# Cross-attention and ternary FFN on one core: the last slot's quantising order, and tile 31 transposed by TensorE

## The reference

```python
# x (8,512,512) f32, ctx (8,64,512), mask (8,64); layernorm without gain, eps 1e-5
x = x + xattn(layernorm(x), ctx, mask)      # softmax over 64 context rows, scale 1/sqrt(512)
x = x + ffn(layernorm(x), w1, g1, w2, g2, w3, g3)
# linear_bit(x, w, g) = act_quant(rmsnorm(x, g)) @ ternary(w).T
#   act_quant: scale = 127 / max|x| of a row; y = round(x * scale) / scale
#   ternary:   s = mean|w|;  wq = round(tanh(w / s)) * arctanh(s)
def ffn(x, ...):
    h = silu(linear_bit(x, w1, g1)) * linear_bit(x, w2, g2)    # 512 -> 2048
    return linear_bit(h, w3, g3)                               # 2048 -> 512
```

## Time and profile before

| | |
|---|---|
| median of 3 runs | 484.7 us (482.98 to 485.55) |
| the profiled execution, its own time | 481.35 us |
| its span in the profile | 479.6 us |
| mean granted TensorE clock | 0.982 |
| busy: PE, DVE, ACT, POOL | 86%, 85%, 73%, 70% |
| DMA transposes into `q3T` | 64, median 3.2 us from issue to landing |

### The profile page before, as it was taken

The page is one execution under the profiler, slowest core; times in us unless marked ns, Lnnn a source line. Parts: engine busy times, 40 slices in busy tenths (PEclk is TensorE's granted clock), DMA queues, the critical chain, the costliest instruction groups (busy, mean ns, idle before and its releaser), DMA issues. The chain is left out here.

```text
span 479.6 us, 8317 instructions
## 1 busy us (share of the span) xinstructions
PE 412.8 (86%) x1910; PEld 195.2 (41%) x1910; DVE 406.7 (85%) x913; ACT 351.0 (73%) x608; POOL 337.5 (70%) x535
## 2 busy tenths in 40 slices
PE   0634777799999999999999999999999999799964
PEld 0511532234634463446344644464345534344421
DVE  3496796989999999999999999999999999987650
ACT  1678669986898769876988698868887876565560
POOL 0146837897877787788778878778777878877540
PEclk9999996999999999999999999999999999999988
DMA  7997661444566455745584557456744334535324
GB/s 265 392 392 249 200 250 22 131 90 110 133 155 165 96 109 153 186 87 124 139 179 87 118 156 175 87 116 179 175 88 111 77 79 92 107 72 99 73 68 87
DMA packets 112616, 67.98 MB, mean 142 GB/s; under 512 B 102864, under 2 KB 102992, under 8 KB 108880
## 3 DMA queue, kind: packets, MB, share of 16 engines
q1 hardware_dynamic: 112592, 67.72, 54.0%
HBM read 34.14 MB, written 8.39 MB: 89 GB/s over the span
## 5 line engine op out<-in xcount | busy, mean ns | idle before, releaser
L488 POOL TENSOR_TENSOR stageB<-stageB,g3b 128x512 f32<-128x512 f32 x128 | 164.1, 1287 | 52.3 <-DVE stageB L855 51.5
L1078 PE MATMUL S<-W2q,q12T 128*128 128x512 f16 x512 | 136.6, 391 | 9.9 <-DVE stageB L855 6.7
L1078 PE MATMUL S<-W1q,q12T 128*128 128x512 f16 x512 | 136.0, 389 | 3.9 <-ACT sg L654 2.4
L1090 PE MATMUL DN<-W3q,stageB 128*128 128x512 f16 x512 | 119.7, 387 | 16.1 <-DMA stageB<-stageB 12.8
L654 ACT ACTIVATE sg<-S,asc 128x512 f32<-128x512 f32 x128 | 87.7, 686 | 58.0 <-PE S L1078 50.9
L855 DVE TENSOR_TENSOR stageB<-sg,S 128x512 f32<-128x512 f32 x128 | 87.0, 680 | 13.7 <-ACT sg L654 8.2
L861 DVE TENSOR_REDUCE hm<-stageB 128x1 f32<-128x512 f32 x128 | 86.7, 679 | 1.7 <-POOL stageB L488 1.7
L1090 PEld LDWEIGHTS DN<-W3q,stageB 128*128 128x128 f16 x512 | 49.5, 99 | 80.6 <-issue 23.2
L1078 PEld LDWEIGHTS S<-W2q,q12T 128*128 128x128 f16 x512 | 49.7, 100 | 78.0 <-DVE stageB L855 15.9
L1078 PEld LDWEIGHTS S<-W1q,q12T 128*128 128x128 f16 x512 | 49.6, 101 | 70.7 <-issue 9.9
L661 ACT ACTIVATE junk<-stageB 128x1024 bf16<-128x1024 f32 x64 | 67.4, 1053 | 7.7 <-DVE stageB L855 7.0
(11 more groups left out here) (95 smaller groups left out, 400.6 us busy)
## 6 DMA issues: line engine op xcount, KB each, us to landing
xTs<-in_xT SPq DMA_DIRECT2D x8, 1024.0 KB, 7.1
X<-in_x SPq DMA_DIRECT2D x8, 1024.0 KB, 7.0
out_x<-X SPq DMA_DIRECT2D x32, 256.0 KB, 3.0
X<-in_w1T SPq DMA_DIRECT2D x4, 1024.0 KB, 12.5
stageB<-in_w2T SPq DMA_DIRECT2D x4, 1024.0 KB, 20.8
X<-in_w3T SPq DMA_DIRECT2D x4, 1024.0 KB, 6.5
ctxr<-in_ctx SPq DMA_DIRECT2D x16, 128.0 KB, 3.0
ctxc<-in_ctx SPq DMA_DIRECT2D x8, 128.0 KB, 4.3
```

Of the source, the lines that this page charges most:

```text
L488: nc.gpsimd.tensor_tensor(gh[q][:, part], hp[:, part], g3b[:, part], ALU.mult).then_inc(s_gh_made, 1)
L1078: mm = nc.tensor.matmul(bank[n % 2][:, :], q12T[q][:, i * KD + k, :], w[:, n, k, :], start=(k == 0), stop=(k == KD - 1))
L1090: mm = nc.tensor.matmul(DN[:, :], q3T[:, k, :], W3q[:, k, :], start=(k == 0), stop=(k == KH - 1))
```

## The change

In the last slot, ACT quantises both halves of tile 30 after `silu(31, 0)` and ahead of `silu(31, 1)`; before, it did this after `silu(31, 2)`.

Tile 31's two DMA transposes are gone. After `down(30)`, TensorE transposes the 16 blocks of `c3`, each 128 x 128 f16, with the f16 identity `ident16` as the moving operand, into three banks read as f16: the blocks 0 to 7 go to `S1[0]`, 8 to 11 to `S1[1]`, 12 to 15 to `S2[0]`. DVE copies the blocks 0 to 3, 4 to 7 and 8 to 11 from PSUM to `q3T`, after `result(30)`; ACT copies 12 to 15 after its quantising. `down(31)` waits for a copy at k = 0, 4, 8 and 12. `ident16` is made on DVE near the start by a cast of `identf`, which POOL makes.

```diff
+        ident16 = sb("ident16", [P, P], F16)
...
+        q3P = [bank[:, :].bitcast(F16) for bank in (S1[0], S1[1], S2[0])]
... SP, after the last slot
-            for h in range(NHALF):
-                transpose_3(NT - 1, h)
... ACT, slot
+                closing = last and j == TPB - 1
+                if closing:
+                    for h in range(NHALF):
+                        quantize_3(t - 1, h, (j - 1) % 2)
                 silu(t, 1, j % NZ)
...
-                if old:
+                if old and not closing:
                     for h in range(NHALF):
                         quantize_3(t - 1, h, (j - 1) % 2)
... ACT, after the last slot
                 quantize_3(NT - 1, h, (NT - 1) % 2)
+            act.wait_ge(s_q3_ps, 3)
+            nc.scalar.copy(q3T[:, 3 * HB // 2:, :].rearrange("p k q -> p (k q)"), q3P[2][:, 0:CH]).then_inc(s_q3_act, 1)
... DVE, start
             nc.vector.memset(ones[:, :], 1.0).then_inc(s_const_ones, 1)
+            dve.wait_ge(s_ident_f, 1)
+            nc.vector.tensor_copy(ident16[:, :], identf[:, :]).then_inc(s_ident_h, 1)
             dve.wait_ge(s_mask_in, 32)
... DVE, end
-            for t in range(NT - 2, NT):
-                worth_3(t, t % 2)
-                result(t)
+            worth_3(NT - 2, NT % 2)
+            result(NT - 2)
+            for i in range(3):
+                if i % 2 == 0:
+                    dve.wait_ge(s_q3_ps, i // 2 + 1)
+                nc.vector.tensor_copy(q3T[:, i * HB // 2:(i + 1) * HB // 2, :].rearrange("p k q -> p (k q)"),
+                                      q3P[i // 2][:, i % 2 * CH:(i % 2 + 1) * CH]).then_inc(s_q3_dve, 1)
+            worth_3(NT - 1, (NT - 1) % 2)
+            result(NT - 1)
... PE
+            def turn_3(t):
+                pe.wait_ge(s_ident_h, 1)
+                for h in range(NHALF):
+                    pe.wait_ge(s_c3_made, NHALF * t + h + 1)
+                    for k in range(h * HB, (h + 1) * HB):
+                        bank, place = (2, k - 3 * HB // 2) if k >= 3 * HB // 2 else (h, k - h * HB)
+                        mm = nc.tensor.transpose(q3P[bank][:, place * P:(place + 1) * P], c3[:, k * P:(k + 1) * P],
+                                                 ident16[:, :])
+                        if k in (HB - 1, 3 * HB // 2 - 1, KH - 1):
+                            mm.then_inc(s_q3_ps, 1)
+
-            def down(t):
+            def down(t, turned=False):
...
                 for k in range(KH):
-                    if k % HB == 0:
+                    if turned:
+                        if k == 3 * HB // 2:
+                            pe.wait_ge(s_q3_act, 1)
+                        elif k % (HB // 2) == 0:
+                            pe.wait_ge(s_q3_dve, k // (HB // 2) + 1)
+                    elif k % HB == 0:
                         pe.wait_ge(s_q3_in[k // HB], 16 * (t + 1))
...
             down(NT - 2)
-            down(NT - 1)
+            turn_3(NT - 1)
+            down(NT - 1, True)
```

More of the change, by code:

```diff
@@ L167, in bit_ffn_xattn @@
         s_ident_f = sem("ident_f")
+        s_ident_h = sem("ident_h")
         s_mask_in = sem("mask_in")
@@ L256, in bit_ffn_xattn @@
         s_q3_in = [sem(f"q3_in_{h}") for h in range(NHALF)]
+        s_q3_ps = sem("q3_ps")
+        s_q3_dve = sem("q3_dve")
+        s_q3_act = sem("q3_act")
         s_down_ps = sem("down_ps")
```

## The result

The changed kernel took 477.91 us (median of 7 runs, 475.92 to 479.48), the kernel before 484.68 (median of 7, 480.87 to 485.55): ratio 0.9884, 95% interval 0.9855 to 0.9912, which is 4.3 to 7.0 us faster, by the middle 5.6 (the two medians themselves lie 6.8 apart). The forecast was 480.2 us, 4.5 faster, with a range from 477.6 to 482.9.

What follows compares the result with a forecast made beforehand. The last slot and its drain were taken as the bound, with TensorE twice behind a DMA and slow projections. The steps end down(31) at 471.3 instead of 475.83, -4.5 us: 484.7 - 4.5 = 480.2 us, range 477.6 to 482.9.

Steps and rivals of the forecast that it cites:

- Step 1: Last slot: tile 30 quantised ahead of silu(31, 1); down(30) ends at 461.9 instead of 466.14, gate(31, 3) starts 0.63 us earlier.
- Step 2: TensorE transposes tile 31 after down(30): 0.15 us per transpose, running from 464.15 to 466.55.
- Step 3: Copies of tile 31's quarters from PSUM, 0.69 us each on DVE and ACT, lie beside TensorE's work and cost nothing.
- transposes that take over 0.2 us each: Sign of being wrong, for TensorE's transposes of tile 31, expected at 0.15 us each, 16 in some 2.4 us.
- the prediction's sign was 0.6 to 0.7: Sign of being right: tile 31's copies take 0.6 to 0.7 us and are done before TensorE asks.
- Step 4: Last projection, down(31), partly at the low clock: 4.7 us, between 4.1 and 5.3, ending at 471.3 instead of 475.83.
- the full clock 15%: Rival: clock stays up after TensorE's 2.25 us pause, down(31) takes 3.61 us; -6.2 us, 478.5 us; 15%.
- The cast: Making ident16 on DVE near the start costs nothing, inside the mask DMA's wait; without that idle about 0.2 us.
- The span: Sign of being right: the profiled span, 479.6 us before, becomes 4 to 5 us shorter.
- Slower: Outcome given 5%; its rival: TensorE's transposes run serially at the low clock, +2.4 us, 487.1 us, 4%.
- no change: Whole-kernel outcome within 0.5%, 2.4 us, given 15%; its no-gain rival, saving lost in earlier slots' shifts: 484.7 us, 5%.

Runs made afterwards that it cites:

- paced DMAs: Versions with each DMA transpose replaced by a non-turning DMA, another 256 KB transfer issued ahead of it; the kernel before so altered: stretch 25.85 us, timed 477.60 us.
- plain DMAs: Versions with each DMA transpose replaced by a DMA of the same 128x1024 f16 that doesn't turn it; the kernel before so altered: stretch 23.74 us, timed 474.63 us.
- the transposes alone: Only TensorE's transposes and the copies, tile 30 quantised in the old place: stretch 20.41 us with plain DMAs, 21.07 us with paced DMAs.
- the pause filled: Changed kernel with plain DMAs plus 512-column matmuls (9, and one between the transposes' halves) in TensorE's last pause: stretch 20.32 us, timed 470.94 us.
- the quantising split: Changed kernel with paced DMAs, DVE quantising tile 31's first half beside ACT's second, plus 7 matmuls in TensorE's pause: stretch 19.72 us, timed 472.38 us.
- the control: Kernel before the change, each DMA transpose replaced by a paced, non-turning DMA: stretch 25.85 us, timed 477.60 us; unpaced: stretch 23.74 us, timed 474.63 us.
- both edits: Changed kernel (early quantising and TensorE's transposes) with its remaining DMA transposes replaced by non-turning DMAs: stretch 20.18 us with paced DMAs, 21.55 us with plain DMAs.

## Why the prediction was right

Every place below is counted from the start of tile 29's down projection; the forecast's are those of its text less 449.46, the measured ones the trace's less 452.64.

| | forecast | measured |
|---|---|---|
| silu(31, 1) starts | 5.20 | 5.20 |
| tile 30's projection | 8.84 to 12.44 | 8.63 to 12.25 |
| gate(31, 3) starts | 9.04 | 8.88 |
| tile 31's quantising starts | 13.47 | 13.18 |
| transposes start, end | 14.69, 17.09 | 14.48, 16.31 |
| the last projection takes, behind the transposes | 4.75 | 4.88 |
| last matmul ends | 21.84 | 21.19 |

The stretch ended 0.65 us sooner than forecast: the transposes began 0.21 us sooner and took 0.57 less, and the projection took 0.13 more.

- **Step 1** held: tile 30's projection closed up behind the up projection and took 3.6. Tile 31's scale was expected 0.63 us earlier and is 0.92 earlier. Two sizes were off: the delay of gate(31, 1) is 0.45 us, not 0.62, because before it had waited for the matmuls and not for the silu; and POOL's root had stood behind the square on ACT, whose end moved too.
- **Step 2** was the mis-sized term: I took 0.15 us for a transpose, and eight took 0.61 us at the full clock, 0.88 mostly at the low one. Instead of 2.4 us of work they are 1.49, and between them TensorE waits 0.34 us for the second half, which I had ready. So what limits them is ACT's quantising.
- By the Trainium skill, "TensorE: Matmul & The Clock Gate", Part 4 (PE-mode transpose), a 128x128 bf16 transpose took about 275 ns in a kernel. The trace is near it for the duration of one instruction, 247 ns on the mean, here f16. It isn't the pace, since the instructions overlap. For the same reason the prediction's own sign of being wrong, "transposes that take over 0.2 us each", is met by the duration of one and not by the time that 16 take:

```profile
L1106 PE MATMUL S<-ident,stageB 128*128 128x128 f16 x16 | 1.5, 247 | 2.6 <-ACT stageB L650 2.6
L1029 DVE COPY stageB<-S 128x512 f16<-128x512 f16 x3 | 1.2, 420 | 1.1 <-PE S L1106 1.1
```

- **Step 3** held: no matmul of the last projection waits for a copy. The copies take 0.42 us on DVE and 0.59 on ACT, not 0.69 (the prediction's sign was 0.6 to 0.7).
- **Step 4** held at 4.88 us between the bounds of 4.1 and 5.3, and that is in part luck: the forecast had the clock fall behind a pause of 2.25 us, and gave the full clock 15%. With paced DMAs it stayed full at the same pause. Had it stayed full here, the end would have come some 1.7 us sooner by the same code's time in that run, and the gain on the stretch would be 6.9 us, still inside the interval. Which of the two the other six timed executions had, no trace shows.
- **The cast** lies inside the wait for the mask, 0.23 us at 1.51 us.
- **The span** was to be 4 to 5 us shorter and was 1.9 shorter in the two profiled executions, mostly because tile 29's projection started 3.2 us later, behind the two low stretches ahead of the change; the timed runs and the stretch show the gain.
- The prediction did not say how much each of the two parts gives, and the runs show that the two waits behind a DMA weigh unequally. The DMA of tile 31 stood on the path; tile 30's early projection in itself releases nothing. It gains through tile 31's earlier scale (0.92 us in the kernel, by the two traces, 0.11 and 0.90 in the experiments) and can lose as much through the pause that it opens (1.23 us in one).
- Slower was given 5% and no change 15%; neither came. Of the 5.6 us by the ratio, 5.2 are the stretch, and the rest lies within the interval. The measured median, 477.91, is near the low end of the range.

What stays open: the parts were measured with plain DMAs, never with DMA transposes. What the transposes alone would give in the kernel itself I can only work out: tile 30's projection would end 16.7 us into the stretch as before, and transposes and projection at the full clock take 5.03: 21.7 against 21.2. That was not tried. Nor were doubled copies, and the versions with the pause filled or the quantising split were only run with rows that are not turned, so none of them is shown to be a better kernel.

## What to carry to other kernels

In the drain at a program's end, moving work earlier pays only if something waits for it; a projection that ends sooner in front of the same late input just lengthens the pause, and a pause on TensorE can be paid again in the matmuls behind it (here up to 5.9 us for 16 that take 3.6 at the full clock). Where blocks of 128x128 must be turned at the end of a dependent chain and TensorE would stand still anyway, its transposes and a copy beat the DMA's latency of 3 to 4 us: the sixteen took 1.8 us here with the wait between them, and the copies hid behind the next matmuls. To compare two kernels whose time scatters by more than the change, measure in both traces the stretch that the change touches, from one same instruction to another.

## What was unexpected of the hardware

- Behind the same pause of TensorE the clock fell in some executions and stayed in others. In the last slot four traces have a pause of 2.22 or 2.23 us: behind it the clock fell in one, the changed kernel, and stayed in three, all paced (the control, the transposes alone, both edits). There, behind 1.77 us and less it stayed and behind 2.73 and more it fell, each time. Near 93 us, in work that no version changes, TensorE waits 2.12 to 2.15 us for W3 in all eleven traces; the eight matmuls behind it took 2.08 us in five of them and 3.57 in six. And ahead of tile 26's projection the clock stayed behind 2.45 us (before) and fell behind 2.15 (after).
- So a part of the tail's length changes from execution to execution: with the paced DMAs the same code behind the scale took 1.7 us less (from the start of `hf` to the last matmul 6.63 us against 8.31). What decides it, these traces don't show.
- A plain DMA of 128x1024 f16 inside SBUF landed in 2.3 us, a DMA transpose of as much in 3.2. With plain DMAs a kernel with the old order was 10 us shorter in all (474.63 against 484.83 for the kernel before in the same set, ratio 0.9798, 0.975 to 0.9845).
- A copy of 128x512 f16 out of PSUM takes DVE 0.42 us, where the gate with one f32 operand in PSUM takes 0.69.
